# A drive for two steps at once in an SSM scan, and the layer-norm rows of three groups in another order

## The reference

```python
xB = einsum('bsd,nd->bsn', x, B)                  # drive of the scan, 128 states
state = tanh(state @ A.T + xB[t])                 # one step after the other
y = x + einsum('bsn,dn->bsd', states, C) + D * x
x = layernorm(x + layernorm(y) * gamma + beta)
scores = sigmoid(x @ router_weight.T)             # 8 experts in 2 groups of 4
# the expert group with the greater sum of its top two, in it the two best experts,
# their scores divided by their sum -> comb
routed = sum_e comb[e] * (silu(x @ w_gate[e]) * (x @ w_up[e])) @ w_down[e]
shared = (silu(x @ sw_gate) * (x @ sw_up)) @ sw_down
out = layernorm(x + routed + shared)
```

## Time and profile before

| | us |
|---|---|
| median of 3 runs | 354.01 (353.46 to 354.36) |
| the profiled execution's own time | 353.79 |
| its span | 352.0 |
| PE busy | 302.4 (86%) |
| DVE busy | 221.0 (63%) |
| POOL busy | 207.3 (59%) |
| ACT busy | 185.6 (53%) |

### The profile page before, as it was taken

How to read it: one execution, slowest core, us unless ns; L and a number is a source line. 1 busy time by engine, 2 the same in 40 slices (tenths; PEclk the granted TensorE clock), 3 DMA queues, 4 the chain that set the end, 5 groups by cost and what they waited for, 6 DMA issues and landing times.

```text
span 352.0 us, 7374 instructions
## 1 busy us (share of the span) xinstructions
PE 302.4 (86%) x2255; PEld 227.5 (65%) x2255; DVE 221.0 (63%) x671; ACT 185.6 (53%) x442; POOL 207.3 (59%) x326
## 2 busy tenths in 40 slices
PE   5999999946696777998998899899899799998940
PEld 4998888846475664764765656476566556787830
DVE  2235998965563893797599499679835723453520
ACT  2565322645357176358349637756864853545420
POOL 8898012453323448648937984678864655578632
PEclk9999999985689986999999999999999999999995
DMA  6992000000000000000000000000001000011001
GB/s 188 343 339 99 0 3 0 2 0 0 0 4 0 2 2 0 19 15 2 0 33 2 2 30 32 2 32 32 0 17 47 3 32 30 7 57 60 32 4 34
DMA packets 6810, 13.19 MB, mean 37 GB/s; under 512 B 1000, under 2 KB 3568, under 8 KB 6768
## 3 DMA queue, kind: packets, MB, share of 16 engines
q1 hardware_dynamic: 5232, 8.47, 7.5%
q0 software_dynamic: 1536, 4.20, 3.4%
HBM read 8.47 MB, written 4.19 MB: 36 GB/s over the span
## 4 chain that ended last, share of the span: by engine, by line
PE 46%; DVE 23%; issue 8%; ACT 7%; POOL 5%; SPq 5%; DMA 2%; ACTq 2%; POOLq 0%; DVEq 0%
PE bank L449 18%; PE bank L472 8%; PE bank L356 5%; PE bank L362 4%; DVE st L964 3%; SPq L290 3%; PE bank L392 3%; PE bank L374 2%; DVE wg L1125 2%; DMA xres<-in_L_attn_x_dram 2%; DVE wu L1129 2%; PE bank L385 2%; POOL out_dram L1382 2%; ACT comb_sorted L740 2%; ACTq L717 2%
## 5 line engine op out<-in xcount | busy, mean ns | idle before, releaser
L1338 POOL TENSOR_TENSOR h<-wu,h 128x512 f16<-128x512 f32 (+1 forms) x54 | 51.0, 947 | 64.0 <-ACT h L756 63.7
L449 PE MATMUL bank<-xT,wg 128*128 x324 | 66.9, 346 | 10.9 <-issue 5.0
L747 ACT ACTIVATE wg<-bank,g_un 128x512 f32<-128x512 f32 (+1 forms) x54 | 32.1, 594 | 79.5 <-PE bank L449 51.9
L472 PE MATMUL bank<-wd,h 128*128 (+1 forms) x504 | 64.7, 275 | 2.1 <-POOL h L1338 2.1
L449 PE MATMUL bank<-xT,wu 128*128 x324 | 65.4, 340 | 0.0
L472 PEld LDWEIGHTS bank<-wd,h 128*128 128x128 f16 x504 | 47.5, 99 | 9.8 <-POOL h L1338 2.6
L449 PEld LDWEIGHTS bank<-xT,wg 128*128 (+1 forms) x324 | 31.3, 101 | 31.8 <-issue 14.7
L1125 DVE SCALAR_TENSOR_TENSOR wg<-bank,u_un,wg 128x512 f32<-128x512 f32 (+1 forms) x44 | 27.3, 620 | 36.1 <-PE bank L449 15.6
L449 PEld LDWEIGHTS bank<-xT,wu 128*128 (+1 forms) x324 | 32.8, 101 | 24.4 <-issue 1.3
L356 PE MATMUL bank<-xT,BT 128*128 128x128 f32 x256 | 39.8, 278 | 0.0
L731 ACT ACTIVATE xT<-bank 128x512 f32 (+1 forms) x64 | 33.6, 613 | 7.9 <-PE bank L409 7.1
(11 more groups left out here) (186 smaller groups left out, 553.8 us busy)
## 6 DMA issues: line engine op xcount, KB each, us to landing
xres<-in_L_attn_x_dram SPq DMA_DIRECT2D x7, 512.0 KB, 6.1
wd<-in_L_ffn_w_down_dram SPq DMA_DIRECT2D x1, 1024.0 KB, 7.1
xres<-in_L_attn_x_dram SPq DMA_DIRECT2D x2, 256.0 KB, 3.0
out_dram<-wd,row_id POOLq DMA_INDIRECT x16, 2.5
out_dram<-z_odd,row_id POOLq DMA_INDIRECT x16, 2.5
states<-in_L_attn_B_dram SPq DMA_DIRECT2D x1, 128.0 KB, 2.5
D_bc<-in_L_attn_D_dram SPq DMA_DIRECT2D x1, 128.0 KB, 5.0
beta_bc<-in_L_attn_beta_dram SPq DMA_DIRECT2D x1, 128.0 KB, 6.4
```

Of the source, the lines that this page charges most:

```text
L449: last = pe.matmul(ps[:, 0:w], up_rows[which][pw][:, part], x2_sorted[:, k * 2 + px, bass.ds(col, w)], start=first, stop=(k == KT - 1 and ...
L472: last = pe.matmul(ps_y[t // 2][:, (t % 2) * DM:(t % 2 + 1) * DM], h16[:, m % 3, ph, t * P:(t + 1) * P], down_rows[pw][:, rows], start=(fi ...
L747: nc.scalar.activation(sg[:, m % 2, 0:w], ps_g[:, 0:w], ACT.Silu, scale=g_un[:, 0:1]).then_inc(sems.silu_done, 1)
L1338: nc.gpsimd.tensor_tensor(h16[:, m % 3, 1, 0:w], h[:, m % 2, 0:w], h16[:, m % 3, 0, 0:w], ALU.subtract).then_inc(sems.h_low, 1)
```

## The change

Four things are edited. The drive is issued once for two steps, 256 columns wide, into one bank whose two quarters hold the two steps' sums; both halves of a pair of tiles are turned in the even step. On PE the maximum of the weights is turned and spread six steps later, projection 2 leaves the scan, `turn_x2(0)` goes on with less to wait for, `logits(0)` moves into the scan, and `logits(1)` and projection 2 go behind the first unit's `up`. On ACT `normalise(0)` is four tiles at once at step 25 of the second rotation, `normalise(1)` goes behind `scores(0)`, and `keep_turned(1)` and `scores(1)` go behind the comb copies of group 0 and into the first unit. On DVE and POOL the rows of group 0 are taken up to their moments before those of group 1, and group 2's go into pass 0, ten units ahead of their use, as those of the later groups.

```diff
             def drive(s, tile):
 
-                if s % 2 == 0 and s < 2 * FIRST:
+                if s < 2 * FIRST:
                     pe.wait_ge(xT_first, s + 2)
-                elif s % 2 == 0 and s < L:
+                elif s < L:
                     pe.wait_ge(xT_done, s - 2 * FIRST + 2)
                 for k in range(KT):
-                    pe.matmul(ps_scan[s % 2][:, 0:P], BT[:, k, :], xT[:, k, tile, :], start=(k == 0), stop=False)
+                    pe.matmul(ps_scan[(s // 2) % 2][:, 0:2 * P], BT[:, k, :],
+                              xT[:, k, tile:tile + 2, :].rearrange("p j c -> p (j c)"),
+                              start=(k == 0), stop=False, skip_group_check=True)
...
-                pe.matmul(ps_scan[s % 2][:, 0:P], AT[:, :], before, start=False, stop=True).then_inc(scan_mm, 1)
-                if s + 1 < SCAN:
+                pe.matmul(scan_sums(s), AT[:, :], before, start=False, stop=True, skip_group_check=True).then_inc(scan_mm, 1)
+                if s % 2 and s + 1 < SCAN:
                     drive(s + 1, (s + 1) % L)
...
-                    if half and sems is main and g >= 3:
+                    if half and sems is main and g >= 2:
                         pe.wait_ge(main.th_done, g)
...
-                if s < HALVES:
-                    turn_x(FIRST + s // 2, s % 2)
+                if s < HALVES and s % 2 == 0:
+                    for k in range(KT):
+                        turn_x(FIRST + s // 2, k)
...
-                if s == 22:
+                if s == 28:
 
                     pe.wait_ge(wmax_part, 3)
...
-                if s == 24:
+                if s == 30:
...
-                if i == 19:
+                if i == 27:
                     pe.wait_ge(main.y1_done, 4)
-                    project(2, 2 * T4, main)
-                if i == 27:
-                    pe.wait_ge(main.y1_done, 6)
                     turn_x2(0, 0, main)
-            logits(0, main)
-            pe.wait_ge(main.th_done, 1)
-            turn_x2(1, 1, main)
+                if i == 30:
+                    logits(0, main)
             places(0)
             for t in range(T4):
                 permute_main(0, t)
-            logits(1, main)
+            pe.wait_ge(main.th_done, 1)
+            turn_x2(1, 1, main)
             turn_comb(0)
...
             up_main(0)
+            logits(1, main)
+            front_late(-1)
...
-                if 22 <= i < 22 + T4:
-                    normalise(0, 0, main, (i - 22,))
+                if i == 25:
+                    normalise(0, 0, main)
...
-                if i == 29:
+                if i == 28:
                     keep_turned(0, main)
 
+            scores(0, main)
             normalise(1, 1, main)
-            scores(0, main)
-            keep_turned(1, main)
             at = offsets(0)
             for t in range(T4):
                 put(0, t, at)
-            scores(1, main)
             put_comb(0, at)
+            keep_turned(1, main)
...
                     high_rows(g, g % 3, main)
-                    if g > 1:
-                        scores(g, main)
+                    scores(g, main)
...
-            rows(0, 0, main)
-            scale_rows(0, 0, main)
-            rows(1, 1, main)
-            sum_rows(0, 0, main)
-            sum_moments(0, 0, main)
-            scale_rows(1, 1, main)
-            sum_rows(1, 1, main)
-            sum_moments(1, 1, main)
-            rows(2, 2, main)
-            scale_rows(2, 2, main)
-            sum_rows(2, 2, main)
-            sum_moments(2, 2, main)
+            for g in range(2):
+                rows(g, g, main)
+                scale_rows(g, g, main)
+                sum_rows(g, g, main)
+                sum_moments(g, g, main)
...
-                g = due(n, 2 * EP, 3)
+                g = due(n, 2 * EP, 2)
                 if g is not None:
                     rows(g, g % 3, main)
```

More of the change, by code:

```diff
@@ L682, in step @@
                 act.wait_ge(scan_mm, s + 1)
-                nc.scalar.activation(dst, ps_scan[s % 2][:, 0:P], ACT.Tanh).then_inc(scan_tanh, 1)
+                nc.scalar.activation(dst, ps_scan[(s // 2) % 2][:, (s % 2) * P:(s % 2 + 1) * P], ACT.Tanh).then_inc(scan_tanh, 1)
             def normalise(g, par, sems, tiles=range(T4)):
@@ L1173, in _ @@
                     sort_tiles(g)
-                g = due(n, 2 * EP - 1, 3)
+                g = due(n, 2 * EP - 1, 2)
                 if g is not None:
@@ L1177, in _ @@
                     sum_rows(g, g % 3, main)
-                g = due(n, 2 * EP - 2, 3)
+                g = due(n, 2 * EP - 2, 2)
                 if g is not None:
@@ L1383, in send @@
                                                  bounds_check=N - 1, oob_is_err=False).then_inc(sems.out_sent[ring if sems is main else 0], 16)
-            for g in range(2):
-                deviations1(g, g, main)
+            deviations1(0, 0, main)
             deviations2(0, 0, main)
+            deviations1(1, 1, main)
             low_rows(0, 0, main)
```

13 lines of the change are left out of this document (6 added, 7 removed).

## The result

The changed kernel takes 360.99 us (median of 4 runs, 360.41 to 361.9) against 354.19 in the same series, ratio 1.0196 (95% interval 1.0167 to 1.0225): 6.8 us slower. The forecast was 358.2, range 355.3 to 361.5. So the time lies inside the range, near its upper end, and in the part of it (over 360) that had a chance of 0.15. The profiled execution took 360.41, span 358.7, against 352.0.

The account below looks back on a forecast made before the run. Bounds: PE in the first rotation, the A matmul-tanh latency chain in the second, then a DVE-PE-ACT chain. Cumulative shift +0.35 at choice 0, +3.3 at group 1's permute, +4.4 at up(5): 353.8 + 4.4 = 358.2 us, range 355.3 to 361.5.

Parts of the forecast that it names:

- over 360: Whole kernel: case of a lower clock or more of DVE's work on the path, time above 360 us, chance 0.15.
- a pair of steps in the second rotation (1.94): Scan, steps 32 to 63: two steps with one double drive take 1.94 us, against 1.71 before.
- the third rival: Scan: double drive takes about 0.53 us, hidden by tanh; time 354.2; chance 0.07, shared with hidden rows.
- all that the first twenty steps lose, lies in a wait for DMA: First rotation: step 20's turn still waits for input until 28.70, so the earlier steps' losses do not show.
- The term +0.2 at A(28): First rotation: the A matmul of step 28 comes at 36.05 us, against 35.82 before.
- +0.35: Scan's end: choice 0 starts at 77.8 us against 77.43, the longer scan nearly offset by DVE no longer being late.
- Taking 2.5 us of lateness off DVE: Ahead of choice 0: DVE's 2.5 us lateness goes, paid for by a scan 2.8 us later.
- The granted clock is at half until 93.0, four us after up(0) starts in today's trace; with the same I get 94.3.: Start of pass 0: PE's clock returns to full four us after the first up, at 94.3 us.
- The terms from up(0) to the permute, +2.9: Pass 0: group 2's rows on DVE between mask and permute; group 1's permute at 101.6 us against 98.27.
- pass 1 was the right analog: Pass 0, permute to up(5): takes pass 1's 14.2 us instead of pass 0's 13.1, giving 115.8 against 111.37.
- the clock falls more: Pass 0: up blocks at 1.2 GHz cost 1.3 us more a unit, 361 to 362; chance 0.15, shared with DVE.
- the shift was to stay: From unit 5 on: order unchanged on every engine, no fixed-time waits, so the +4.4 us shift stays.

Follow-up runs that it names:

- e3: Changed kernel with the two-step, 256-column drive split in halves over two gaps and x turned one half a step: 356.24 us.
- e1: Changed kernel with the earlier drive, one step of 128 columns behind every A matmul, and x turned one half a step: 356.96 us.
- e2: Kernel before with the two-step, 256-column drive alone: 359.09 us.
- e5: Changed kernel with 28 unread fp16 matmuls of 512 columns in PE's idle stretches between the scan and pass 0: 357.35 us.
- e13: e10 with 25 unread matmuls of 512 columns added as PE filler: 351.44 us, ratio 0.986.
- e11: Changed kernel with logits(1) and projection 2 moved one unit later, behind the second unit's up: 360.68 us.
- e10: Kernel before with VectorE's rows group by group, all ahead of choice 0, and POOL's roots of groups 1 and 2 ahead of group 0's low rows: 351.52 us.
- e12: e10 with the two-step drive split over two gaps: 351.51 us, ratio 0.987.
- e8: Kernel before with the two-step, 256-column drive split over two gaps: 355.34 us, ratio 1.0015.
- e14: Kernel before with only POOL's list changed, group 1's second and group 2's first root ahead of group 0's low rows: ratio 0.996.

## Why the prediction was right, and where its size was off

The forecast was 4.4 us, measured were 6.8. The mechanism was right in the main: the scan grows by the double drive, group 2's rows and the logits cost in pass 0 what pass 1 shows, DVE no longer waits. Two terms were too small, the first rotation's and the clock's in pass 0, and two errors the other way hid part of that.

**The drive.** The price of a 256-column pass (0.216) and of a pair of steps in the second rotation (1.94) came out exactly, and the cheap drive of the third rival did not come: e3 shows that the drive hides only in halves. Shown.

**The first rotation.** The step "all that the first twenty steps lose, lies in a wait for DMA" failed: a pair takes 1.99 us there, not 1.94, the pair with the turns of C and the router 2.37, and the first turn was 0.2 later, so step 20's turn came at 29.25 without a wait. Behind it the prediction's sum is 0.2 short against its own pair: from the turn to the next even A matmul it has 0.44 + 0.21 + 0.86 = 1.51, where 1.94 less the 0.22 up to the turn is 1.72; measured were 1.78. The term +0.2 at A(28) measured +1.2 between these two traces. As before's place moves with the input by a microsecond from trace to trace, the drive's own share is less sure: between the two sets of traces given ahead of e1 the mean distance is 0.9. That the 0.05 us more of a pair is a wait for ACT's copy of xT was read from the rows (the copy ends at 32.00, the drive's weights start to load at 32.05, 0.05 later behind the A matmul than in the second rotation), not tested.

**The end of the scan and choice 0.** DVE idles more than 8 us, as said. A(28) was 1.0 us later than forecast and choice 0 only 0.5 (+0.9 instead of +0.35), for the stretch between them took 41.3 us and not 41.75: one error hid part of the other. "Taking 2.5 us of lateness off DVE" holds as a difference to before. What the prediction did not see is that this lateness hangs on the scan: e2 shows that the double drive alone costs 5.2 us at choice 0, and the changed kernel has 4.3 of them less.

**Pass 0.** The step that failed is "The granted clock is at half until 93.0, four us after up(0) starts in today's trace; with the same I get 94.3." It stayed at half until 101.2. The prediction had carried the clock's return over from a trace in which two units' ups stand there, to a list in which logits(1) does. The terms from up(0) to the permute, +2.9, measured +5.3: to the end of the mask 7.9 us instead of 6.9, from there 6.7 instead of 5.4. e5 shows 3.4 us of the changed kernel's stretch to be half clock, in both logits(1) and projection 2, for whose second half rows(2) waited. By e5 and e13 the +5.3 are 3.0 of list and 2.3 of clock, what the changed order pays beyond what before pays. From permute to up(5) pass 1 was the right analog: 14.36 against 14.24. The rival "the clock falls more" had the right cause at another place, and its time, 361; the chance for all over 360 was 0.15.

**Behind unit 5** the shift was to stay. It shrank by 0.6 us, all of it in pass 2: from up(10) to the next pass it is 29.1 us instead of 29.7. Before's trace has the clock at half for the first 3.8 us of that pass. The two others that have it so (e11, e13) take as long, 29.6 and 29.9; the eleven that do not take 28.9 to 29.4. So before's trace was a little long there, and the forecast has no term for it. Without these 0.6 us the changed kernel's median would have been at about 361.6, just outside the range: that the time fell inside owes as much to luck.

So the 6.7 us are: +0.9 to choice 0, -0.1 to up(0), +5.3 to the permute (3.0 longer list, 2.3 clock), +1.3 to up(5), -0.6 in pass 2. Or by parts of the change: undoing the drive gives 4.0 back; the rest, 356.96 against 354.19, is the move of group 2's rows and logits into pass 0, net of what choice 0 gained. e1 and e10 give that move's price without the gain, since their choices 0 start within 0.3 us of one another (74.71 and 75.03): e1's trace ends 5.1 us later, and its median is 5.4 us higher, in another series. It was not split further: with projection 2 in the scan, banks 6 and 7 would have to be read before group 0's turn, which was not tried.

The better version is e10 (or e12): 351.5 us, about 1% under the kernel before (ratio 0.985 to 0.995), without any of this change's drive and with group 2's rows where they were.

## What to carry to other kernels

Two matmuls that each hid in a gap do not hide as one double matmul in every second gap: count what one gap holds, not the sum. Where an engine is late, follow its wait to the end before you credit its removal; a lateness that hangs on the stage you lengthen grows with it. And take the clock's return from a trace in which PE does the same work at that place, as a guess: what brings it back was not found here.

## What the runs showed of the hardware

**PE busy, clock at half.** In the changed kernel PE worked without a gap from 89.74 us and its granted clock stayed at 0.50 until 101.22, over up(0) (256 columns), 16 logits passes of 8 columns and eight passes of 256. In the three traces with this order and no filler (changed kernel, e1, e3) the clock was back 10.9 to 11.5 us after up(0) began; in the seven in which a second up follows the first (before, e2, e8, e10, e11, e12, e14) 2.7 to 5.6. So the order goes with the return, but it is not shown to be the cause: in e8 and e11 the clock came back within 0.2 us of the second up's start. In e11 it was full from 86.1 to 89.3 while PE was busy for 0.09 us. In e5, with 28 filler matmuls, it did not fall between the scan and 127.4. What decides is not settled by the runs.

**Two groups of times.** 31 runs of the kernel before in one series lie from 352.8 to 354.9 and from 356.9 upwards, with nothing between; in a series of ten others lie between too (355.04 to 356.63), so it is not always so plain. e8 has the same two groups, and its profiled run is one of the upper: its pass 1 takes 29.3 us instead of before's 25.7, with half clock for 10.3 of them:

```profile
112.30:122.60 10.30, 10.30 (x45) 8.47 (x43) 3.42 (x14) 1.92 (x4) 2.94 (x3) 0.50 0.01 2
111.52:140.82 29.30, 23.64 (x159) 19.27 (x160) 18.71 (x71) 14.18 (x35) 13.00 (x28) 0.77 0.00 1
```

e14 has two groups again, six runs from 351.6 to 353.1 and six from 355.2 to 356.3, and its profiled run, too, is one of the upper: pass 1 takes 29.7 us, with half clock for 10.2 of them. In both stretches PE was busy without a gap:

```profile
110.30:120.50 10.20, 10.20 (x44) 8.42 (x43) 2.59 (x12) 1.92 (x4) 2.94 (x3) 0.50 0.01 2
```

The pass is 3.6 to 4.0 us longer than before's, about the distance of the groups (3.4 between their medians in e8, 3.2 in e14). So when the clock falls is likely what makes the groups. It is not shown: no lower run of e8 or e14 was profiled, and no upper run of before.

**VectorE beside GpSimd.** In e10 four scalar_tensor_tensor of 128x256 took 1.66 us alone and 3.54 us beside one GpSimd tensor_tensor of 2.34 us, which itself took 2.13 us in the changed kernel, where no such VectorE work ran beside it, and 2.40 in e2.
